# A GRU recurrence taken per half of its units, with the input products of 32 steps made at a time

## The chip, the core and the metric

One core of a Trainium2 chip runs the whole program. Its engines are named as the profile names them: PE (TensorE, the matmuls, with PEld for the weight loads that run beside them), DVE (VectorE), ACT (ScalarE), POOL (GpSimd) and SP (SyncE, which issues the transfers). The metric is the device time of one execution in microseconds, as the median over runs. Lower is better.

## What is computed

Four layers follow each other, each added to its input: two attention layers, a GRU over 256 time steps with 8 sequences and 512 units, and a layer with a norm. The change is in the third:

```python
def cell(h, x):
    gi = x @ W_ih + b_ih
    gh = h @ W_hh + b_hh
    i_r, i_z, i_n = jnp.split(gi, 3, axis=-1)
    h_r, h_z, h_n = jnp.split(gh, 3, axis=-1)
    r = jax.nn.sigmoid(i_r + h_r)
    z = jax.nn.sigmoid(i_z + h_z)
    n = jnp.tanh(i_n + r * h_n)
    h_new = (1.0 - z) * n + z * h
    return (h_new, h_new)
_, hs = jax.lax.scan(cell, initial_state, xs)
```

`r` is the reset gate, `z` the update gate, `n` the candidate. Each step needs the state of the step before, so 256 steps follow each other.

## The kernel before

The attention layers fill the first 926 us. Then comes `recurrent_and_last_layer`. Each of its 256 steps makes 48 recurrent products (L1003): for each of the three gates, four chunks of 128 of the 512 units of the state (`held`, the stationary side, 8 columns for the 8 sequences) times four blocks of 128 output units. The four blocks go to four groups of 32 partitions of one PSUM bank, so four products stand side by side in the array. The products are fp32; each is written once in the code and stands as two matmuls and two weight loads in the profile, so 48 are 96 and 96.

The banks are `psR` for reset (gate0), `psN` for the candidate (gate1) and `psZ`, two in turn, for the update gate (pg0, pg1). Before the recurrent products of the next step, `begin` (L1005) starts the update bank with its share of the input (`pick` times `foldZ`, L1018; in the first 16 steps L1016 in fp32) and the candidate bank with its bias (L1022), in bf16 of 128 columns.

DVE turns a bank by 32 x 32 blocks (STREAM_TRANSPOSE), so that units lie on the partitions, and then: reset turned (L896) and its input share added (L898), ACT's sigmoid (L951); candidate turned (L901), times reset (L905), plus its input share (L907), ACT's tanh (L953); update turned in two halves (L910, L911), two sigmoids (L956). The new state comes from two scans (L919), one for each half of the units. The next step's first products need the first half only; the wait for the second half stands after 12 of the 48 products.

Between the steps PE makes input products for later steps in the time that the chain leaves it: reset and candidate shares, 16 steps at a time (`TG`), 128 moving columns (`piece`, L977; ACT evicts them at L935), two pieces of four products a step; and update shares (`piece_z`, L987), one piece of four products a step, two in the first 16 steps. The shares of the first 16 steps are all made ahead of step 0. Pieces end 16 steps before the last step for reset and candidate and 32 steps before it for update. In the last 16 steps PE also makes column means for the last layer (L1059, L1066).

POOL adds the state to the residual stream (L855) and sums for the last layer (L859). Every engine runs its instructions in the order in which the code writes them, with semaphores between engines.

Of the kernel before, what the change touches and what calls it, by code (L numbers as in the profile page):

```python
# [680 lines left out]
def recurrent_and_last_layer(nc, xT, kept, loaded, w_hh, wk, wo, rowc, cols, out):  # L681
# [14 lines left out]
    with ExitStack() as ctx:  # L696
# [32 lines left out]
        def chunk(c, blk):  # L729
# [4 lines left out]
        tr = [trn[:, g, :].rearrange("p (c m) -> p c m", c=C)[:, :, 0:B] for g in range(GATES)]  # L734
# [3 lines left out]
        psZ, gb = pg[0:2], pg[2:4]  # L738
        (s_init, s_chain, s_gi_mm, s_gi_ev, s_acc, s_r, s_n) = (
            sem(n) for n in ("gates_cleared", "step_product", "gi_products",  # L740
                             "gi_ready", "state_added", "reset_ready", "candidate_ready"))
# [4 lines left out]
        R, Z, N = 0, 1, 2  # L746
        s_ps = [sem(f"gate_products{g}") for g in (R, N)]
        s_psz = sem("update_products")
        s_tr = sem("gates_turned")
        s_trz = [sem(f"update_turned{a}") for a in range(2)]  # L750
        s_pre = [sem(f"gate_summed{g}") for g in (R, N)]
        s_z = [sem(f"update_ready{a}") for a in range(2)]
        s_h = [sem(f"state_ready{a}") for a in range(2)]
        psR, psN, zb = ps
        NINIT = 22
        tR, tN = 0, 1


        TG, TZ, RZ = 16, 16, 3
        NG, PER = T // TG, 8  # L760
        gru = ctx.enter_context(ExitStack())

        near = gru.enter_context(nc.psum_tensor("near", [P, 512], fp32))
        turnedZ = [x[:, P:P + 64] for x in (psR, near)]
# [30 lines left out]
        T0 = T - TG  # L795
# [3 lines left out]
        with nc.Block() as block:  # L799
            @block.sync  # L800
            def _(sp):
# [8 lines left out]
                for n in range(1, NZ):  # L810

                    sp.wait_ge(s_part, 6 * n)
                    if n > RZ:

                        sp.wait_ge(s_psz, TZ * (n - RZ + 1))
# [46 lines left out]
            def _(dve):  # L862
# [5 lines left out]
                for bank in psZ:  # L868
                    dve.memset(bank[:, 0:P], 0.0).then_inc(s_init, 1)
                dve.memset(psN[:, 0:P], 0.0).then_inc(s_init, 1)  # L870
# [19 lines left out]
                for t in range(T):  # L890
# [4 lines left out]
                    dve.wait_ge(s_ps[tR], t + 1)  # L895
                    dve.transpose(trn[:, R, :], psR[:, 0:P]).then_inc(s_tr, 1)  # L896
                    dve.wait_ge(s_tr, 2 * t + 1)
                    dve.tensor_tensor(pre[:, 0], tr[R], share(t, R), ALU.add).then_inc(s_pre[tR], 1)  # L898

                    dve.wait_ge(s_ps[tN], t + 1)  # L900
                    dve.transpose(trn[:, N, :], psN[:, 0:P]).then_inc(s_tr, 1)  # L901

                    dve.wait_ge(s_tr, 2 * t + 2)
                    dve.wait_ge(s_r, t + 1)
                    dve.tensor_tensor(tmp[:], tr[N], rg[:], ALU.mult).then_inc(s_chain, 1)  # L905
                    dve.wait_ge(s_chain, t + 1)
                    dve.tensor_tensor(pre[:, 1], tmp[:], share(t, N), ALU.add).then_inc(s_pre[tN], 1)  # L907

                    dve.wait_ge(s_psz, t + 1)
                    dve.transpose(turnedZ[0], psZ[q][:, 0:64]).then_inc(s_trz[0], 1)  # L910
                    dve.transpose(turnedZ[1], psZ[q][:, 64:128]).then_inc(s_trz[1], 1)  # L911

                    for a in range(2):
                        dve.wait_ge(s_z[a], t + 1)
                        if a == 0:
                            dve.wait_ge(s_n, t + 1)
                            if t > 1:
                                dve.wait_ge(s_acc, t - 1)
# [8 lines left out]
            def _(a):  # L927
# [20 lines left out]
                for t in range(T):  # L948
                    q = t % 2
                    a.wait_ge(s_pre[tR], t + 1)  # L950
                    a.activation(rg[:], pre[:, 0], ACT.Sigmoid).then_inc(s_r, 1)  # L951
                    a.wait_ge(s_pre[tN], t + 1)
                    a.activation(sides[q][:, :, :, 0:3:2], pre[:, 1].rearrange("p c (b v) -> p c b v", v=1).to_broadcast([P, C, B, 2]), ACT.Tanh).then_inc(s_n, 1)  # L953
                    for z in range(2):
                        a.wait_ge(s_trz[z], t + 1)
                        a.activation(by[:, half(z), :, 2], turnedZ[z].rearrange("p (c m) -> p c m", c=H)[:, :, 0:B], ACT.Sigmoid).then_inc(s_z[z], 1)  # L956
# [11 lines left out]
            def _(pe):  # L968
# [31 lines left out]
                def products(bank, g, q, c, first, done, lo=0, hi=P):  # L1000
                    for j in range(4):
                        o = g * D + P * j
                        last = pe.matmul(bank[32 * j:32 * j + B, lo:hi], held[q][:, c, :], whh[:, c, o + lo:o + hi], start=first, stop=done)  # L1003
                    return last
                def begin(t):  # L1005

                    n, v = t // TZ, t % TZ
                    if t == 0:
                        pe.wait_ge(s_z0, 1)
                    elif n > 0 and v == 0:  # L1010
                        pe.wait_ge(s_zd[n % RZ], 192 * (n // RZ + (0 if n % RZ == 0 else 1)))
                    if t > 1:
                        pe.wait_ge(s_trz[1], t - 1)
                    for j in range(4):
                        if n == 0:
# [398 lines left out]
```

## Time and profile before

| | before |
|---|---|
| median of 3 runs | 1963.13 us (1960.36 to 1968.94) |
| profiled execution, span | 1963.7 us (the page gives no other time for it) |
| PE busy | 1832.6 us, 93% |
| PE weight loads busy | 1269.7 us, 65% |
| DVE busy | 1147.7 us, 58% |
| ACT busy | 785.3 us, 40% |
| mean granted TensorE clock | 0.968 |

Busy shares are over the whole span; the change touches only the stretch from 926 us on. In a table of stretches each engine has its busy time and, in brackets, its instructions. In a listing in order of time each row is a run of like instructions: start, length of the run, engine, line, operation, output and inputs, shapes, count, and in square brackets the idle time of the engine just before and what ended it. "issue" there means that nothing which the profile shows was waited for. PE's row and PEld's row of one line are the matmuls and the weight loads of the same products.

### The profile page before, as it was taken

To read this page: it belongs to the slowest core of one execution; us is meant where nothing else is said; L and a number is where in the kernel's file an instruction comes from. 1 tells how busy PE (TensorE), PEld (TensorE's weight loads), DVE (VectorE), ACT (ScalarE), POOL (GpSimd) and SP (SyncE) were. 2 spreads that over 40 slices of the span, in tenths; PEclk is the share of its full clock that TensorE was granted. 3 is DMA by queue.
4 is the path that set the end of the run, shared out by engine and by line. 5 is a ranking of instruction groups with operands and counts; after the bars stand their busy time and mean duration, and the time that the engine had idled before them with its cause. 6 is when DMAs were issued, how large, how long until landed. Compare 5 with 4: busy or idle time off the path is not lost. (4 is left out here: it accounts for less than half of the span.)

```text
span 1963.7 us, 85507 instructions
## 1 busy us (share of the span) xinstructions
PE 1832.6 (93%) x37682; PEld 1269.7 (65%) x37682; DVE 1147.7 (58%) x3364; ACT 785.3 (40%) x2196; POOL 393.5 (20%) x862
## 2 busy tenths in 40 slices
PE   6999999999999999988999999999999999999983
PEld 2433444453444344444998888888888999888861
DVE  5667676766676667343455555555555555555567
ACT  0554565655555565633222222222222222222224
POOL 0121211121111212110122122221222211222113
PEclk7997999999999999989999999999999999999995
DMA  6654443526152623141100000000000000000002
GB/s 160 219 141 126 121 127 85 152 63 181 47 172 67 180 68 93 34 152 42 77 15 10 13 13 13 13 4 13 13 13 13 7 11 13 13 13 12 5 4 86
DMA packets 65377, 127.65 MB, mean 65 GB/s; under 512 B 15401, under 2 KB 22057, under 8 KB 61412
## 3 DMA queue, kind: packets, MB, share of 16 engines
q1 hardware_dynamic: 61372, 120.30, 21.3%
q8 instruction: 296, 4.85, 1.0%
q0 software_dynamic: 3072, 0.82, 0.2%
q10 hardware_dynamic: 560, 1.05, 0.2%
q14 instruction: 77, 0.63, 0.1%
HBM read 77.56 MB, written 37.85 MB: 59 GB/s over the span
## 5 line engine op out<-in xcount | busy, mean ns | idle before, releaser
L439 DVE TENSOR_REDUCE mx<-MX 128x1 f32<-128x512 f32 x768 | 483.3, 683 | 191.7 <-PE MX L568 191.2
L1003 PE MATMUL gate<-whh,state 128*8 128x128 f32 x16384 | 503.8, 273 | 31.5 <-DVE state L919 13.4
L504 ACT ACTIVATE pr<-ST 128x512 f32<-128x512 f32 x768 | 409.5, 596 | 223.5 <-PE ST L588 223.1
L1003 PEld LDWEIGHTS gate<-whh,state 128*8 128x8 f32 x16384 | 430.4, 91 | 87.6 <-DVE state L919 84.7
L896 DVE STREAM_TRANSPOSE trn<-gate 128x128 f32<-128x128 f32 x256 | 81.3, 318 | 337.7 <-PE gate L1003 337.7
L1003 PE MATMUL pg<-whh,state 128*8 128x128 f32 x8192 | 278.4, 273 | 0.3 <-issue 0.3
L951 ACT ACTIVATE rg<-pre 128x32 f32<-128x32 f32 x256 | 58.8, 230 | 504.0 <-DVE pre L898 504.0
L568 PE MATMUL MX<-K,Q 51*128 51x512 f32 (+1 forms) x768 | 242.4, 445 | 15.0 <-DMA Q<-d_q 10.5
L588 PE MATMUL ST<-Q,K 53*128 53x512 f32 (+1 forms) x768 | 240.6, 485 | 13.3 <-ACT pr L504 9.2
L588 PEld LDWEIGHTS ST<-Q,K 53*128 53x128 f32 (+1 forms) x768 | 98.7, 189 | 215.5 <-ACT pr L504 118.9
L1003 PEld LDWEIGHTS pg<-whh,state 128*8 128x8 f32 x8192 | 230.3, 90 | 1.2 <-issue 0.9
L855 POOL TENSOR_TENSOR xT<-xT,state 128x32 f32<-128x32 f32 x256 | 67.4, 263 | 730.9 <-DVE state L919 730.9
L977 PE MATMUL pg<-xT,wih 128*32 128x128 f32 x4096 | 183.4, 276 | 12.0 <-issue 10.6
L568 PEld LDWEIGHTS MX<-K,Q 51*128 51x128 f32 (+1 forms) x768 | 121.1, 196 | 75.7 <-DVE mx L439 42.8
L382 POOL TENSOR_TENSOR nmp<-nm,zero 16x128 fp32r<-16x128 f32 x48 | 21.5, 448 | 629.3 <-ACT nm L520 629.3
L604 PE MATMUL AV<-pr,va 128*17 128x512 f32 x1024 | 139.0, 615 | 0.9 <-ACT pr L504 0.9
L977 PEld LDWEIGHTS pg<-xT,wih 128*32 128x32 f32 x4096 | 117.6, 110 | 25.3 <-issue 23.6
L953 ACT ACTIVATE state<-pre 128x64 f32<-128x64 f32 x256 | 66.5, 260 | 164.5 <-DVE pre L907 164.5
L919 DVE TENSOR_TENSOR_SCAN state<-by,state 128x48 f32<-128x48 f32 x512 | 104.5, 246 | 33.0 <-ACT by L956 0.5
L987 PE MATMUL gate<-wihZ,xT 128*32 128x128 f32 x2048 | 112.5, 273 | 1.4 <-PEq L33 1.4
L901 DVE STREAM_TRANSPOSE trn<-gate 128x128 f32<-128x128 f32 x256 | 81.0, 316 | 24.6 <-PE gate L1003 0.7
L910 DVE STREAM_TRANSPOSE gate<-pg 128x64 f32<-128x64 f32 x256 | 67.9, 265 | 24.8 <-PE pg L1003 0.6
(190 smaller groups left out, 1943.3 us busy)
## 6 DMA issues: line engine op xcount, KB each, us to landing
d_q<-hi_q SPq DMA_DIRECT2D x32, 256.0 KB, 3.5
d_q<-lo_q SPq DMA_DIRECT2D x32, 256.0 KB, 4.0
d_k<-hi_k SPq DMA_DIRECT2D x32, 256.0 KB, 2.9
d_k<-lo_k SPq DMA_DIRECT2D x32, 256.0 KB, 2.9
K<-d_k SPq DMA_DIRECT2D x64, 128.0 KB
Q<-d_q SPq DMA_DIRECT2D x64, 128.0 KB
K<-d_k SPq DMA_DIRECT2D x16, 512.0 KB
Q<-d_q SPq DMA_DIRECT2D x16, 512.0 KB
```

The lines of the kernel that those rows point to most:

```text
L439: dve.reduce_max(mx[:, u, col:col + 1], bank[:, :], AX.X).then_inc(mx_red, 1)
L504: act.activation(pr[:, kc % 2, i], ST[n % 3][:, :], ACT.Exp, scale=SCALE[UNITS[w][0]]).then_inc(exped, 1)
L568: pe.matmul(bank[:, :], Q[r, h, tok(qb)], K[r, h, :], start=True, stop=True).then_inc(mx_mm, 1)
L588: pe.matmul(ST[n % 3][:, :], K[r, h, tok(kc)], Q[r, h, :], start=True, stop=True).then_inc(st_mm, 1)
L604: last = pe.matmul(AV[r, :], v, pr[:, kc % 2, i, :], start=kc == 0, stop=kc == KC - 1)
L896: dve.transpose(trn[:, R, :], psR[:, 0:P]).then_inc(s_tr, 1)
L901: dve.transpose(trn[:, N, :], psN[:, 0:P]).then_inc(s_tr, 1)
L910: dve.transpose(turnedZ[0], psZ[q][:, 0:64]).then_inc(s_trz[0], 1)
L919: dve.tensor_tensor_scan(state[:, 1 - q, W3 * a:W3 * a + W3], by[:, half(a)].rearrange("p c b v -> p (c b v)"), threes(q, a), 0.0, ALU.mul ...
L977: last = pe.matmul(gb[i % 2][32 * j:32 * j + 32, 0:TG * B], wih[:, n, i * P + 32 * j:i * P + 32 * j + 32], xT[:, n, TG * blk:TG * (blk + 1 ...
L987: last = pe.matmul(zb[32 * j:32 * j + 32, P * w:P * (w + 1)], xT[:, k, t0:t0 + 4, :].rearrange("p t b -> p (t b)"), wihZ[:, k, P * w:P * ( ...
L1003: last = pe.matmul(bank[32 * j:32 * j + B, lo:hi], held[q][:, c, :], whh[:, c, o + lo:o + hi], start=first, stop=done)
```

## The change

The recurrent weights are put in another order on the host (`by_half`): the reset gate first, then for the first half of each 128-unit block its candidate and update columns side by side, then the same for the second half. A bank then holds 64 candidate and 64 update columns of one half: `psA` (gate1) for the first, `psB` (pg0, pg1 in turn) for the second. One step now makes reset and first-half products of the near chunks of the state, waits for the state's second half after 16 of the 48 products (before: 12), makes the far chunks of both, and then the whole second half. DVE turns each half's bank whole, and both the candidate's arithmetic and ACT's tanh run once for each half. The bank `near` goes.

The input shares of reset and candidate are made for 32 steps at a time (`TG` 32), 256 moving columns, one piece of four products a step instead of two; the first 32 steps' shares are made ahead of step 0, and the pieces end 32 steps before the last step. ACT's evictions come every fourth step instead of every second. Starting the banks takes 16 matmuls of 64 columns instead of 8 of 128.

```diff
-        TG, TZ, RZ = 16, 16, 3
+        TG, TZ, RZ = 32, 16, 3
...
+                    def turn(a):
+                        dve.wait_ge(s_ps[a], t + 1)
+                        dve.transpose(trn[:, a, :], half_bank(a, t)[:, 0:P]).then_inc(s_tr[a], 1)
+                    def candidate(a):
+                        dve.wait_ge(s_tr[a], t + 1)
+                        if a == 0:
+                            dve.wait_ge(s_r, t + 1)
+                        dve.tensor_tensor(tmp[:, half(a)], tr[a][:, 0:H], rg[:, half(a)], ALU.mult).then_inc(s_chain, 1)
+                        dve.wait_ge(s_chain, 2 * t + a + 1)
+                        dve.tensor_tensor(pre[:, 1, half(a)], tmp[:, half(a)], share(t, N)[:, half(a)], ALU.add).then_inc(s_pre[a], 1)
+                    def update(a):
                         dve.wait_ge(s_z[a], t + 1)
+                        dve.wait_ge(s_n[a], t + 1)
...
+                    turn(0)
+                    candidate(0)
+                    turn(1)
+                    update(0)
+                    candidate(1)
+                    update(1)
...
-                    if blk + 1 < NG and k % 2 == 1:
-                        keep(blk + 1, k // 2)
+                    if blk + 1 < NG and k % 4 == 3:
+                        keep(blk + 1, k // 4)
...
+                def begin(t, a):
...
                     for j in range(4):
+                        o = P * j + HW * a
+                        pe.matmul(bank[32 * j:32 * j + B, 0:HW], ones_b[:], bnp[:, o:o + HW], start=True, stop=False)
                     for j in range(4):
+                        o = P * j + HW * a
...
+                        pe.matmul(bank[32 * j:32 * j + B, HW:P], pick[:, B * (v % 4):B * (v % 4) + B], foldZ[:, n % RZ, v // 4, o:o + HW], start=False, stop=False)
...
                     if t > 0:
                         pe.wait_ge(s_h[0], t)
+                        pe.wait_ge(s_trr, t)
+                    products(psR, 0, q, NEAR, first=True)
+                    products(psA, 1, q, NEAR)
                     if t > 0:
                         pe.wait_ge(s_h[1], t)
+                    products(psR, 0, q, FAR, done=True).then_inc(s_psr, 1)
+                    products(psA, 1, q, FAR, done=True).then_inc(s_ps[0], 1)
+                    products(psB[q], 2, q, range(C), done=True).then_inc(s_ps[1], 1)
...
-                        piece(blk + 1, 2 * k)
-                        piece(blk + 1, 2 * k + 1)
+                        piece(blk + 1, k)
```

PE in one step of the recurrence, from the starting of the next step's banks to the update products. In these rows a fp32 product counts once. Before:

```order
L1018 MATMUL pg1<-foldZ,pick 8x128 [waits update_turned1]
L1018 MATMUL pg1<-foldZ,pick 8x128 x3
L1022 MATMUL gate1<-bnp,ones_b 8x128 [waits gates_turned]
L1022 MATMUL gate1<-bnp,ones_b 8x128 x3
L977 MATMUL pg2<-xT,wih_49 32x128 [waits gi_ready]
L977 MATMUL pg2<-xT,wih_49 32x128 x7
L987 MATMUL gate2<-wihZ,xT 32x128 x4
L1003 MATMUL gate0<-whh,state 8x128 [waits state_ready0]
L1003 MATMUL gate0<-whh,state 8x128 x7
L1003 MATMUL gate1<-whh,state 8x128 x4
L1003 MATMUL gate0<-whh,state 8x128 [waits state_ready1]
L1003 MATMUL gate0<-whh,state 8x128 x7
```

PE at the same place after the change:

```order
L1027 MATMUL gate1<-bnp,ones_b 8x64 [waits half_turned0]
L1027 MATMUL gate1<-bnp,ones_b 8x64 x3
L1033 MATMUL gate1<-foldZ,pick 8x64 x4
L1027 MATMUL pg1<-bnp,ones_b 8x64 [waits half_turned1]
L1027 MATMUL pg1<-bnp,ones_b 8x64 x3
L1033 MATMUL pg1<-foldZ,pick 8x64 x4
L984 MATMUL pg3<-xT,wih_49 32x256 [waits gi_ready]
L984 MATMUL pg3<-xT,wih_49 32x256 x3
L994 MATMUL gate2<-wihZ,xT 32x128 x4
L1011 MATMUL gate0<-whh,state 8x128 [waits reset_turned,state_ready0]
L1011 MATMUL gate0<-whh,state 8x128 x7
L1011 MATMUL gate1<-whh,state 8x128 x8
```

Sixteen narrow products start the banks instead of eight wide ones, four wide input products stand for eight, and the step's first product waits for two signals.

DVE in one step before, from the candidate's turning to the two scans (printed as SCALAR_TENSOR_TENSOR):

```order
L901 STREAM_TRANSPOSE trn<-gate1 128x128 [waits gate_products2]
L905 TENSOR_TENSOR tmp<-trn,rg 128x32 [waits reset_ready,gates_turned]
L907 TENSOR_TENSOR pre<-tmp,giT 128x32 [waits step_product]
L910 STREAM_TRANSPOSE gate0<-pg0 128x64 [waits update_products]
L911 STREAM_TRANSPOSE near<-pg0 128x64
L919 SCALAR_TENSOR_TENSOR state<-by,state 128x48 [waits state_added,candidate_ready,update_ready0]
L919 SCALAR_TENSOR_TENSOR state<-by,state 128x48 [waits update_ready1]
```

DVE at the same place after the change:

```order
L904 STREAM_TRANSPOSE trn<-gate1 128x128 [waits half_products0]
L910 TENSOR_TENSOR tmp<-trn,rg 128x16 [waits reset_ready,half_turned0]
L912 TENSOR_TENSOR pre<-tmp,giT 128x16 [waits step_product]
L904 STREAM_TRANSPOSE trn<-pg0 128x128 [waits half_products1]
L919 SCALAR_TENSOR_TENSOR state<-by,state 128x48 [waits state_added,candidate_ready0,update_ready0]
L910 TENSOR_TENSOR tmp<-trn,rg 128x16 [waits half_turned1]
L912 TENSOR_TENSOR pre<-tmp,giT 128x16 [waits step_product]
L919 SCALAR_TENSOR_TENSOR state<-by,state 128x48 [waits candidate_ready1,update_ready1]
```

The first half's scan now stands ahead of the second half's candidate, and behind the turning of the second bank.

## Rows read from the trace of the kernel before

**Rows 1.** The page: span, engines (busy us, share, instructions), a transfer queue (packets, MB).

```profile
span 1963.7 us, 85507 instructions
...
PE 1832.6 (93%) x37682; PEld 1269.7 (65%) x37682; DVE 1147.7 (58%) x3364; ACT 785.3 (40%) x2196; POOL 393.5 (20%) x862
...
q8 instruction: 296, 4.85, 1.0%
```

**Rows 2.** Table of stretches, reset transposes (L896) alone: one a step.

```profile
942.20:1006.50 64.30, 5.08 (x16) 1.00 0.04 12
1006.50:1787.10 780.60, 66.07 (x208) 1.00 0.04 11
1787.10:1903.00 115.90, 9.85 (x31) 1.00 0.03 8
```

**Rows 3.** Stretches: length, busy us and instructions of PE, PEld, DVE, ACT, POOL.

```profile
942.20:1006.50 64.30, 62.73 (x2252) 59.99 (x2242) 32.72 (x144) 18.15 (x75) 13.88 (x37) 1.00 0.04 12
1006.50:1787.10 780.60, 753.98 (x26627) 696.82 (x26624) 421.92 (x1873) 208.60 (x950) 174.38 (x494) 1.00 0.04 11
1251.90:1344.30 92.40, 87.72 (x3073) 80.96 (x3073) 48.80 (x217) 24.21 (x110) 20.93 (x58) 1.00 0.05 13
```

**Rows 4.** In order of time, one undisturbed step of the recurrence.

```profile
1058.64 1.65 PEld L1003 LDWEIGHTS gate<-whh,state 128*8 128x8 f32 x64 [0.40 <-DVE state L919]
1058.64 1.94 PE L1003 MATMUL gate<-whh,state 128*8 128x128 f32 x64
...
1059.99 0.32 DVE L896 STREAM_TRANSPOSE trn<-gate 128x128 f32<-128x128 f32 x1 [1.26 <-PE gate L1003]
...
1060.34 0.19 DVE L898 TENSOR_TENSOR pre<-trn,giT 128x32 f32<-128x32 f32 x1
1060.39 1.06 PE L1003 MATMUL pg<-whh,state 128*8 128x128 f32 x32
1060.56 0.23 ACT L951 ACTIVATE rg<-pre 128x32 f32<-128x32 f32 x1 [1.84 <-DVE pre L898]
...
1061.27 0.24 PE L1018 MATMUL pg<-foldZ,pick 96*8 96x128 bf16 x4
...
1061.38 0.62 PE L977 MATMUL pg<-xT,wih 128*32 128x128 f32 x16
1061.44 0.26 ACT L953 ACTIVATE state<-pre 128x64 f32<-128x64 f32 x1 [0.65 <-DVE pre L907]
1061.52 0.27 DVE L910 STREAM_TRANSPOSE gate<-pg 128x64 f32<-128x64 f32 x1
1061.69 0.22 DVE L911 STREAM_TRANSPOSE near<-pg 128x64 f32<-128x64 f32 x1
...
1062.04 0.41 DVE L919 TENSOR_TENSOR_SCAN state<-by,state 128x48 f32<-128x48 f32 x2
1062.35 0.23 PEld L1003 LDWEIGHTS gate<-whh,state 128*8 128x8 f32 x12 [0.40 <-DVE state L919]
```

**Rows 5.** In order of time, weight loads after a pause in three successive steps.

```profile
1274.48 0.25 PEld L977 LDWEIGHTS pg<-xT,wih 128*32 128x32 f32 x9 [0.66 <-issue]
...
1278.23 0.25 PEld L977 LDWEIGHTS pg<-xT,wih 128*32 128x32 f32 x9 [0.38 <-issue]
...
1282.25 0.25 PEld L977 LDWEIGHTS pg<-xT,wih 128*32 128x32 f32 x9 [0.66 <-issue]
```

**Rows 6.** Waits of weight loads (total us, times, longest): first 16 steps; then 208.

```profile
PEld gate L1003 <- issue: 1.8, 3, 0.8
...
PEld gate L1003 <- DVE state L919: 60.7, 164, 0.5
PEld pg L977 <- issue: 20.2, 46, 0.7
```

**Rows 7.** In order of time, PE's input products ahead of step 0.

```profile
934.22 5.37 PE L977 MATMUL pg<-xT,wih 128*32 128x128 f32 x128 [2.35 <-issue]
940.15 2.06 PE L977 MATMUL pg<-xT,wih 128*32 128x128 f32 x67 [0.56 <-issue]
```

More of the change, by code:

```diff
@@ L733, in recurrent_and_last_layer @@
         trn = sb("trn", [P, GATES, P])
-        tr = [trn[:, g, :].rearrange("p (c m) -> p c m", c=C)[:, :, 0:B] for g in range(GATES)]
+        tr = [trn[:, i, :].rearrange("p (c m) -> p c m", c=C)[:, :, 0:B] for i in range(3)]
         pre = sb("pre", [P, 2, C, B])
@@ L867, in _ @@
                 dve.memset(state[:], 0.0).then_inc(s_init, 1)
-                for bank in psZ:
+                for bank in psB:
                     dve.memset(bank[:, 0:P], 0.0).then_inc(s_init, 1)
-                dve.memset(psN[:, 0:P], 0.0).then_inc(s_init, 1)
+                dve.memset(psA[:, 0:P], 0.0).then_inc(s_init, 1)
                 dve.memset(ones_b[:], 1.0).then_inc(s_init, 1)
@@ L913, in _ @@
-                    for a in range(2):
+                    dve.wait_ge(s_psr, t + 1)
+                    dve.transpose(trn[:, 2, :], psR[:, 0:P]).then_inc(s_trr, 1)
+                    dve.wait_ge(s_trr, t + 1)
+                    dve.tensor_tensor(pre[:, 0], tr[2], share(t, R), ALU.add).then_inc(s_prer, 1)
+                    def turn(a):
+                        dve.wait_ge(s_ps[a], t + 1)
+                        dve.transpose(trn[:, a, :], half_bank(a, t)[:, 0:P]).then_inc(s_tr[a], 1)
@@ L998, in _, with products @@
                 pe.wait_ge(s_init, NINIT)
-                def products(bank, g, q, c, first, done, lo=0, hi=P):
-                    for j in range(4):
[L1002 to L1013, printed above, removed]
+                def products(bank, part, q, chunks, first=False, done=False):
+                    for c in chunks:
+                        for j in range(4):
+                            o = part * D + P * j
+                            last = pe.matmul(bank[32 * j:32 * j + B, 0:P], held[q][:, c, :], whh[:, c, o:o + P], start=first and c == chunks[0], stop=done and c == chunks[-1])
+                    return last
@@ new lines, in begin @@
+                def begin(t, a):
+                    n, v = t // TZ, t % TZ
+                    bank = half_bank(a, t)
+                    if a == 0:
+                        if t == 0:
+                            pe.wait_ge(s_z0, 1)
+                        elif n > 0 and v == 0:
+                            pe.wait_ge(s_zd[n % RZ], 192 * (n // RZ + (0 if n % RZ == 0 else 1)))
+                    if t > a:
+                        pe.wait_ge(s_tr[a], t - a)
+                    for j in range(4):
+                        o = P * j + HW * a
+                        pe.matmul(bank[32 * j:32 * j + B, 0:HW], ones_b[:], bnp[:, o:o + HW], start=True, stop=False)
@@ L1019, in begin @@
-                    if t > 0:
-                        pe.wait_ge(s_tr, 2 * t)
-                    for j in range(4):
-                        pe.matmul(psN[32 * j:32 * j + B, 0:P], ones_b[:], bnp[:, P * j:P * (j + 1)], start=True, stop=False)
-                begin(0)
+                        pe.matmul(bank[32 * j:32 * j + B, HW:P], pick[:, B * (v % 4):B * (v % 4) + B], foldZ[:, n % RZ, v // 4, o:o + HW], start=False, stop=False)
+                begin(0, 0)
+                begin(0, 1)
+                NEAR, FAR = range(H), range(H, C)
```

83 lines of the change are left out of this document (29 added, 54 removed).

## The prediction

> **What bounds the kernel now.** I read the page's head first, then the table of stretches, then one step in order of time, then the waits of the weight loads. The page [rows 1] gives 1963.7 us for the span and one number that decides this forecast: the queue of instruction packets moved 296 packets of 4.85 MB in all, 16 KB each, while PE ran 37,682 matmuls and 37,682 weight loads. 75,364 / 296 = 255, so one packet feeds about 256 PE instructions. I call that a block.
>
> The recurrence takes 256 steps, from about 942 to 1906 us. The count of reset transposes [rows 2] splits them: 16 first steps in 64.30 us (4.02 each), 208 steps in 780.60 us (3.753 each), then 31 in 115.9 us (3.74 each). In the 208 steps PE runs 26,627 + 26,624 instructions [rows 3], 256 a step, exactly one block a step.
>
> An undisturbed step [rows 4] takes 3.71 us (first product at 1058.64, next at 1062.35), and its end is a chain: 96 product matmuls, turn the update gate, sigmoid, scan, next product. PE idles 0.40 us on its weight port before the next step, until the scan lets it go. So the chain sets that step. Yet over the 208 steps the weight port sat idle 60.7 us for the scan and 20.2 us on "issue" [rows 6]: it waited for nothing the profile can name. Those pauses (46 of them) all stand at the input products, and in three successive steps they lie 3.75 and 4.02 us apart [rows 5]. Among the input products made ahead of the recurrence two such pauses stand exactly 128 matmuls, and so 128 loads, apart [rows 7]: the edge of a block. I read them as PE waiting for its next block of instructions. In the first 16 steps the weight port never waits for the scan; its waits are four lines of "issue", 3.5 us together, of which the longest stands in [rows 6]. PE is wanted all the time, at a granted clock of 1.00, and 2252 + 2242 instructions, 17.55 blocks, took 64.30 us: 3.66 us a block [rows 3].
>
> So there are three limits close together: the chain (3.71), PE's own work (below, 3.42), and the supply of blocks (3.66 and more).
>
> **The change part by part.** *The chain.* A group of four matmuls, one for each quarter of the partitions, takes 0.109 us (64 in 1.75 us, 1058.64 to 1060.39 [rows 4]). The reset transpose starts 1.35 us after the first product, 0.26 after its 40 matmuls are through. After the change reset is complete after 48: 1.31 + 0.26 = 1.57. Transpose to addition 0.35, addition to sigmoid 0.22, sigmoid 0.23 + 0.03: reset ready at 2.40. The first half's bank is complete after 64: 2.01, turned by 2.37. Product, addition and tanh of half the width: I take 0.22, 0.23 and 0.26 as for the full width (a little high): 3.1. On VectorE the scan of this half stands behind the transpose of the second bank, which waits for all 96 products (2.88). That transpose takes 0.32, but the row of the half transposes shows the next instruction 0.17 after one of 0.27, so the scan starts between 3.1 and 3.2. From scan to product 0.31: **3.41 to 3.51** against 3.71. The second half follows from 3.28 with product, addition, tanh and scan (0.22 + 0.22 + 0.26 and then 0.31), so PE sees its state at about 4.3; PE asks for it 32 matmuls after its own start, 0.87 us after 3.41 to 3.51, so at 4.28 at the earliest: in time, or 0.05 late.
>
> *PE's own work.* The weight port, idle for 0.40 until 1062.35, had its last load under way at 3.31 after the start [rows 4]; with one more group of 0.109 PE is through at 3.42 of 3.71. The starts of the banks go from two groups of 128 columns, 0.055 us each (1061.27 to 1061.38), to four groups of 64. No row shows 64 columns. If the columns set it, four cost the same 0.11; if each group has the price of the wide one, 0.22. So 0 to +0.11; I take +0.03, nearer the first, since the fp32 groups of [rows 4] too are paced by their columns (0.109 us for twice 0.055). The input products go from four groups of 128 columns to two of 256: columns alike, 0. PE's work is 3.41 to 3.53.
>
> *Instructions.* This is the term that counts. Of the rows PE runs in a step, 16 go with the input products (8 matmuls and 8 loads fewer) and 16 come with the halved starts. Still 256. The first product now waits for two signals; no row shows what a second wait is, and I count it as one instruction more: 257. In the first 16 steps, where the update share enters in fp32, 2 x 144 + 1 = 289 against 4494 / 16 = 281. So the change asks for 16 x 289 / 256 + 208 x 257 / 256 = 226.9 blocks where 844.9 us are spent today.
>
> *What a block costs* when PE wants it at once: 3.66 us in the first 16 steps, the only stretch where PE never waits for the chain; 3.753 over the 208 steps, which is too high as it holds the 60.7 us for the scan; 3.85 in the worst stretch of 92.4 us, 24.0 blocks [rows 3]. I take 3.71, between the first two. 226.9 x 3.71 = 841.8 us: **-3.1 us**. The chain's gain of 0.2 to 0.3 us a step turns into longer waits for blocks.
>
> The Trainium skill, "Runtime: NRT & Kernel Launch", section "Instruction fetch mechanics", says that instructions are refilled in blocks of 256, which the trace agrees with, and that crossing an edge is mostly hidden, since an engine dispatches more slowly than blocks arrive. The 20.2 us of "issue" speak against that second part here. By it the sum would be that of the first rival.
>
> *The last 32 steps* have no input products and no update products, so 224 + 1 instructions: a block lasts 1.14 steps, 3.71 / 1.14 = 3.26, under the chain. Here the gain is real: 3.74 - 3.47 = 0.27 in 28 of them. Three more hold a 512-column mean product, with which PE itself sets the step, and in the very last the second half ends about 0.4 later. 7.5 - 0.4 is about **-7.0**, bounds -2 and -9.
>
> *Ahead of the recurrence* the first input products now cover 32 steps: 256 matmuls of 256 columns, 64 groups at 0.213 instead of 0.109, +6.7. Among those of before PE idles 2.35 and 0.56 on issue [rows 7], which the longer work can fill: +6.7 - 2.9 = **+3.8**, bounds 0 and +7. ScalarE's evictions are half as many and twice as wide, VectorE has ten instructions a step for nine; both are idle for over a third of the 780.6 us [rows 3], so this costs 0 while PE sets the step; without that cover it is the 0.05 above.
>
> Sum: -3.1 - 7.0 + 3.8 = -6.3, on the profiled span of 1963.7: 1957.4. That span is 0.6 over the median of 1963.13, so **1957 us**.
>
> **The rivals.** *Blocks are not a limit.* Then a step takes the longer of chain and PE's work, 3.41 to 3.53, middle 3.47: 208 x (3.753 - 3.47) = 59 less, the pauses of 3.5 us in the first steps go too, and with -7.0 + 3.8 it is 1963.7 - 65.7 = 1898 us. For it: the undisturbed stretch has no pauses at 3.71 us a step. Against it: the first 16 steps, which want a block each 3.49 us (32 groups of 0.109) and get one each 3.66. The rule of the Trainium skill's "Runtime: NRT & Kernel Launch" given above is this rival's.
>
> *Blocks come as in the worst stretch.* After a pause PE has no lead, so the next block is late again; the intervals of 3.75 and 4.02 [rows 5] are then the rule. Today the wait for the scan gives a late block time to arrive; the change takes that wait away. At 3.85 a block: 226.9 x 3.85 = 873.6, +28.7, in all +25.5: 1989 us. The point of decision: with x us a block the sum is 226.9 x - 844.9 - 3.2; it is zero at 3.738, 0.5% over at 3.781 and 0.5% under at 3.695. Against it: that stretch is the worst of the trace.
>
> *The early start does not come.* The first half's scan stands behind the second bank's transpose. If the half-width steps cost more than I think and the chain stays at 3.71, the last steps gain nothing: 1964 us.
>
> **How the numbers follow.** 0.5% (about 10 us) is what a measurement of this kernel can tell from no change. Forecast (blocks at 3.66 to 3.78): 0.74, 1946 to 1973. Blocks no limit: 0.13. Blocks at 3.78 or more: 0.09. No early start: 0.04. Within the forecast I put 0.37 below 3.695. Faster: 0.13 + 0.74 x 0.37 = 0.40; slower 0.09; same the rest, 0.51. The range leaves out the first rival's 0.13 and the upper half of the second: 1938 to 1976.
>
> **What would show it.** In the changed profile: still one instruction packet for about 256 PE instructions; in the 208 steps 50 to 60 us of "issue" on the weight port instead of 20.2, and under 15 us for the scan instead of 60.7; the 208 steps in 765 to 785 us; the pauses no longer at one place in the step, since 257 instructions shift the edge by one each step; 31 last steps in about 109 us; the first product of the recurrence 4 us later. The forecast is wrong if issue time stays near 20 us while the scan's wait falls: then 1898 it is. It is wrong the other way if pauses of 4.02 follow each other through the stretch.

## The result: a little slower, 1.0068 of the time before

The changed kernel takes 1975.92 us (median of 20 runs) where the kernel before takes 1960.38 on the same chip (20 runs): a ratio of 1.0068, 95% interval 1.005 to 1.0086. In a second set of runs it was 1.0058 (1.0031 to 1.0084). So it is slower by some 6 to 17 us. The forecast was 1957 us, 6 less than before: the sign is wrong. The time lies inside the range that was given, 1938 to 1976, but only by 0.1 us, which is luck; by the prediction's own mark of 0.5% it is the outcome "slower", to which it gave 0.09.

The head of the page of the kernel after, to set beside [rows 1]:

```profile
span 1980.4 us, 86586 instructions
...
PE 1850.9 (93%) x37746; PEld 1216.0 (61%) x37746; DVE 1202.7 (61%) x3620; ACT 851.3 (43%) x2388; POOL 393.7 (20%) x862
...
q8 instruction: 297, 4.87, 1.0%
```

There are 64 matmuls and 64 loads more than before, and one packet more: still 75,492 / 297 = 254 PE instructions a packet. The stretches are those of [rows 2] (first 16 steps, 208 steps, the rest; the last row holds 32 reset turns here and 31 there, so the two aren't to be compared). Columns as in [rows 3]: length, busy us and instructions of PE, PEld, DVE, ACT, POOL, granted clock, DMA share, GB/s:

```profile
954.30:1019.00 64.70, 63.07 (x2312) 58.48 (x2302) 33.94 (x157) 21.29 (x85) 13.06 (x36) 1.00 0.04 11
1019.00:1803.00 784.00, 761.46 (x26649) 646.05 (x26643) 468.98 (x2083) 262.19 (x1106) 174.63 (x494) 1.00 0.05 11
1803.00:1919.00 116.00, 99.05 (x3578) 86.90 (x3574) 76.45 (x326) 37.72 (x161) 21.71 (x70) 1.00 0.03 8
```

The 208 steps take 784.0 us for 780.6, although PE's weight port is busy 51 us less than before. What it waits for in these steps (the five largest of eleven lines: total us, times, longest), beside [rows 6]:

```profile
PEld gate L1011 <- DVE state L919: 45.1, 158, 0.6
PEld gate L1027 <- DVE trn L904: 15.4, 33, 0.6
PEld pg L1011 <- issue: 7.2, 19, 0.7
PEld gate L1011 <- issue: 5.1, 14, 0.6
PEld pg L984 <- issue: 3.6, 9, 0.6
```

Before, all 46 pauses on "issue" stood at the input products. Now they stand at many places of the step (all lines of issue together 22.4 us). The second wait ahead of the step's first product (`s_trr`, L1041) stands in PE's queue as an instruction of its own, once a step, so that a step has 257; the kernel before has none there. In the 208 steps (line, times, ns, first and last start):

```profile
L1041 PEldq EVENT_SEMAPHORE  x208: 51/51/51, 1022.7 to 1802.2; - x104
```

With these counted, all 52 pauses of over 0.2 us on issue stand whole multiples of 256 instructions apart, to within one instruction. So they are edges of blocks.

There is also a new wait: PE starts a bank (L1027) and waits until VectorE has turned the first half (L904). Its cause is in the time order of a step. First an undisturbed step of the kernel after, beside [rows 4]:

```profile
1124.51 2.03 PE L1011 MATMUL gate<-whh,state 128*8 128x128 f32 x64
...
1126.15 0.32 DVE L897 STREAM_TRANSPOSE trn<-gate 128x128 f32<-128x128 f32 x1 [0.80 <-PE gate L1011]
...
1126.73 0.23 ACT L957 ACTIVATE rg<-pre 128x32 f32<-128x32 f32 x1 [1.36 <-DVE pre L899]
...
1127.46 0.32 DVE L904 STREAM_TRANSPOSE trn<-pg 128x128 f32<-128x128 f32 x1
1127.48 0.23 ACT L962 ACTIVATE state<-pre 128x32 f32<-128x32 f32 x1 [0.30 <-DVE pre L912]
...
1127.80 0.26 DVE L919 TENSOR_TENSOR_SCAN state<-by,state 128x48 f32<-128x48 f32 x1
...
1128.11 0.23 PEld L1011 LDWEIGHTS gate<-whh,state 128*8 128x8 f32 x12 [0.20 <-DVE state L919]
```

From first product to first product it is 3.60 us. The scan of the first half starts 0.34 after the second bank's transpose, when that has ended; and the reset turn starts 1.64 after the first product. Now a step in which GpSimd works on the update shares (L835):

```profile
1081.28 1.28 POOL L835 TENSOR_TENSOR giZ<-giZ,bz 128x512 f32<-128x512 f32 x1
1081.45 0.32 DVE L897 STREAM_TRANSPOSE trn<-gate 128x128 f32<-128x128 f32 x1 [0.87 <-PE gate L1011]
...
1081.80 0.81 DVE L899 TENSOR_TENSOR pre<-trn,giT 128x32 f32<-128x32 f32 x1
```

The reset addition, 0.19 us in the undisturbed step, takes 0.81 and ends as GpSimd's instruction ends (1082.61 and 1082.56). So it is with all 43 of these additions that take over 0.26 us: each ends 0.045 to 0.050 us after a long instruction of GpSimd. The transpose, which reads the bank, keeps its 0.32. Over all 256 steps the line's shortest, median and longest durations in ns are:

```profile
L899 DVE TENSOR_TENSOR pre<-trn,giT x256: 191/193/928, 956.4 to 1918.9; 128x32 f32<-128x32 f32 x128
```

It happens in three of every 16 steps. These take 4.24, 4.18 and 4.19 us on average, the other thirteen 3.56 to 3.73. GpSimd waits for the state's second half before it adds it up, and its long instruction stands behind those adds. The second half now comes later in the step, and so the long instruction falls on the reset addition, which is on the chain. In the kernel before, the two overlapped less: the additions of the 208 steps were lengthened by 5.0 us in all there, and by 25.1 here. This agrees with the Trainium skill, "SBUF — State Buffer", section "SBUF: two separate sides": a VectorE instruction with two SBUF inputs and a GpSimd instruction that reads SBUF exclude each other for their whole length.

So two things could hold the 208 steps at 784 us: the supply of instruction blocks (**theory B**), or the delays by GpSimd (**theory A**: 39 steps of about 0.6 us, some 25 us), without which the changed chain would have paid.

### The profile page after: what moved, and what is told of

Its sections match the earlier page's. It is cut to its first block and busy times, and to the rows that moved or that the text cites. A ratio compares the mean times of both kernels' runs of the same rounds, so it can differ in the third digit from the quotient of the medians.

```text
span 1980.4 us, 86586 instructions
## 1 busy us (share of the span) xinstructions
PE 1850.9 (93%) x37746; PEld 1216.0 (61%) x37746; DVE 1202.7 (61%) x3620; ACT 851.3 (43%) x2388; POOL 393.7 (20%) x862
## 5 line engine op out<-in xcount | busy, mean ns | idle before, releaser
L1011 PE MATMUL gate<-whh,state 128*8 128x128 f32 x16384 | 513.6, 273 | 26.2 <-DVE state L919 22.8
L1011 PEld LDWEIGHTS gate<-whh,state 128*8 128x8 f32 x16384 | 411.0, 91 | 103.7 <-DVE state L919 69.1
L1011 PE MATMUL pg<-whh,state 128*8 128x128 f32 x8192 | 285.7, 273 | 3.1 <-issue 2.7
L897 DVE STREAM_TRANSPOSE trn<-gate 128x128 f32<-128x128 f32 x256 | 81.2, 317 | 218.6 <-PE gate L1011 218.6
L919 DVE TENSOR_TENSOR_SCAN state<-by,state 128x48 f32<-128x48 f32 x512 | 131.5, 257 | 105.8 <-ACT state L962 94.2
L962 ACT ACTIVATE state<-pre 128x32 f32<-128x32 f32 x512 | 118.8, 232 | 166.0 <-DVE pre L912 166.0
L984 PE MATMUL pg<-xT,wih 128*32 128x256 f32 x2048 | 163.0, 381 | 1.5 <-issue 1.2
L960 ACT ACTIVATE by<-trn 128x16 f32<-128x16 f32 x512 | 114.9, 224 | 30.5 <-DVE trn L904 13.6
L910 DVE TENSOR_TENSOR tmp<-trn,rg 128x16 f32<-128x16 f32 x512 | 83.9, 164 | 35.8 <-ACT rg L957 1.0
L912 DVE TENSOR_TENSOR pre<-tmp,giT 128x16 f32<-128x16 f32 x512 | 89.6, 175 | 18.0 <-DVE tmp L910 0.4
```

Source lines behind the costliest of these rows:

```text
L912: dve.tensor_tensor(pre[:, 1, half(a)], tmp[:, half(a)], share(t, N)[:, half(a)], ALU.add).then_inc(s_pre[a], 1)
L960: a.activation(by[:, half(z), :, 2], tr[z][:, H:C], ACT.Sigmoid).then_inc(s_z[z], 1)
L962: a.activation(sides[q][:, half(z), :, 0:3:2], pre[:, 1, half(z)].rearrange("p c (b v) -> p c b v", v=1).to_broadcast([P, H, B, 2]), ACT.T ...
L984: last = pe.matmul(gb[i % 2][32 * j:32 * j + 32, 0:TG * B], wih[:, n, i * P + 32 * j:i * P + 32 * j + 32], xT[:, n, TG * blk:TG * (blk + 1 ...
L1011: last = pe.matmul(bank[32 * j:32 * j + B, 0:P], held[q][:, c, :], whh[:, c, o:o + P], start=first and c == chunks[0], stop=done and c == ...
```

## The experiments

**Take the delays away.** e1 makes the three long additions of GpSimd 16 columns wide and leaves the other columns out; e2 cuts them into quarters of 128 columns over more steps and computes everything.

```diff
e1
-  pool.tensor_tensor(giZ[1][:], giZ[1][:], bz[:, 0], ALU.add)
+  pool.tensor_tensor(giZ[1][:, 0:16], giZ[1][:, 0:16], bz[:, 0, 0:16], ALU.add)
...
-  pool.tensor_tensor(giZ[1][:], giZ[1][:], parts_z[:, i // 2 - 1], ALU.subtract)
+  pool.tensor_tensor(giZ[1][:, 0:16], giZ[1][:, 0:16], parts_z[:, i // 2 - 1, 0:16], ALU.subtract)
e2
+  PART_AT = [(j, w) for j in range(6) for w in (range(C) if j % 2 == 0 else (0,))]
...
+  c = slice(P * w, P * w + P)
...
+  pool.tensor_tensor(giZ[1][:, c], giZ[1][:, c], bz[:, 0, c], ALU.add)
...
+  pool.tensor_tensor(giZ[1][:, c], giZ[1][:, c], parts_z[:, j // 2 - 1, c], ALU.subtract)
```

> The changed kernel, but POOL's three additions and subtractions that split the update shares work on 16 of 512 columns (the other columns are left out, so the shares are incomplete). Theory A: these POOL operations hold up VectorE's reset addition in three steps of each 16 (4.28, 4.18 and 4.18 us a step against 3.56), 2.1 us for each 16 steps, 28 to 30 us in the 208 steps. Then the stretch shrinks from 783.7 to about 757 us, a little more than that if PE's waits for instructions rise, and the kernel is at 0.985 to 0.992 of the changed one, about 1948 us. Theory B (my prediction's: PE's supply of instruction blocks sets the pace at 3.71 us a step, and the long steps only stand where waits for blocks would stand otherwise): the stretch stays over 770 us, the kernel over 1964 us, and 'issue' idle on the weight port doubles from 22 us.

> The changed kernel with the same splitting work on POOL in full, but each addition and subtraction of 512 columns made as four of 128 columns, spread over 12 steps instead of 6. Theory A: each piece takes about 0.45 us and ends about when VectorE's reset addition starts, so the long steps go and the kernel is within 5 us of the narrow one, about 1950 us, faster than both given kernels. Theory B: no more than 5 us gained against the changed kernel. A rival within A, that the delay comes from the total time POOL works beside VectorE and not from where it falls: the four pieces cost as much as the one, spread out, and the kernel stays at about 1976 us.

e1: 1975.24 us, 1.0034 of before (1.0013 to 1.0055). e2: 1975.38 us, 1.005 (1.0028 to 1.0073). The 208 steps took 790.7 and 790.2 us, not fewer than in the kernel after. The waits of e1's weight loads in them:

```profile
PEld pg L1011 <- issue: 20.7, 45, 1.0
PEld gate L1011 <- DVE state L919: 20.4, 90, 0.6
PEld gate L1011 <- issue: 12.1, 31, 1.0
```

The waits for the scan have shrunk to 20.4 us, the wait for the turn is gone, and the nine-line list's eight lines of issue add up to 57.1. The delays were taken away and pauses for blocks took their place; all 114 of over 0.2 us stand multiples of 256 instructions apart. Theory A alone is out, and what was expected by theory B came (over 770 us, over 1964 us, issue more than doubled).

**Each part of the change alone.** e3 is the kernel after with 16-step input products (273 PE instructions a step instead of 257); e4 is the kernel before with 32-step products (240 instead of 256).

```diff
e3
-  TG, TZ, RZ = 32, 16, 3
+  TG, TZ, RZ = 16, 16, 3
...
-  piece(blk + 1, k)
+  piece(blk + 1, 2 * k)
+  piece(blk + 1, 2 * k + 1)
e4
-  TG, TZ, RZ = 16, 16, 3
+  TG, TZ, RZ = 32, 16, 3
...
-  piece(blk + 1, 2 * k)
-  piece(blk + 1, 2 * k + 1)
+  piece(blk + 1, k)
```

> The changed kernel with the input products of reset and candidate made 16 steps at a time with 128 columns, as before: the recurrence per half alone. PE then runs 273 instructions a step instead of 257. Theory A (blocks cost time only where PE asks for them faster than about one each 3.55 us): 273 instructions want a block each 3.34 us, so the undisturbed steps are held up too, at 3.6 to 3.75 us a block or 3.85 to 4.0 us a step, less what the POOL delays already cover: 208 steps take 790 to 815 us, 3.5 us come back ahead of step 0, and the kernel is at 1980 to 2000 us. Theory B, 3.71 us a block throughout: 3.96 us a step, 823 us, about 2010 us. If blocks cost nothing: 1972 us, only the start gained.

> The kernel before with the input products made 32 steps at a time, 256 columns, and nothing else: PE runs 240 instructions a step instead of 256 and wants a block each 3.96 us. Both theories: no 'issue' pauses in the steps, 208 steps at 3.72 us, 774 us instead of 781, and 3 to 4 us more ahead of step 0: about 1956 us, 0.996 to 1.000 of the kernel before. If the pauses are not the supply of instructions: the stretch stays at 780 us and the kernel is 3 us slower.

e3: 2030.75 us, 1.0309 (1.027 to 1.0348); the 208 steps 843.9 us. That is more than any of the three expectations allowed (2010 us at most): a block cost 3.804 us here, not 3.71. e4: 1956.37 us, 0.9947 (0.9918 to 0.9976); the 208 steps 773.0, as expected. All waits of e4's weight loads in its 208 steps are one line:

```profile
PEld gate L1003 <- DVE state L919: 84.9, 209, 0.5
```

No pause is left: at 240 instructions a step lasts 3.715 us, what the undisturbed step of [rows 4] takes. The second half of the change is a gain by itself. The first half, the recurrence per half, costs 63 us in the 208 steps, at 273 instructions each instead of 256.

**The count alone.** e8 adds 16 matmuls of one column to a step of e4 (272 instructions), e10 adds 8 to a step of the kernel after (273). e5 takes 16 instructions away from each step of the kernel after, from step 16 on: each half's bank is started by 4 matmuls of 128 columns, the candidate's bias rows beside the update's shares in one operand.

```diff
e8
+  if TZ <= t < T - 2 * TZ:
+      for i in range(16):
+          pe.matmul(psN[32 * (i % 4):32 * (i % 4) + B, 400:401], ones_b[:], bnp[:, 0:1], start=False, stop=False)
...
e10
+  if TZ <= t < T - 2 * TZ:
+      for i in range(8):
+          pe.matmul(psA[32 * (i % 4):32 * (i % 4) + B, 400:401], ones_b[:], bnp[:, 0:1], start=False, stop=False)
e5
...
+  for j in range(4):
+      o = P * (2 * j + a)
+      pe.matmul(bank[32 * j:32 * j + B, 0:P], pick[:, B * (v % 4):B * (v % 4) + B], foldZ[:, n % RZ, v // 4, o:o + P], start=True, stop=False)
+  return
...
```

> The kernel of e4 (before, with the 256-column input products alone, 240 TensorE instructions a step, 3.715 us a step, no pauses) and, in steps 16 to 223, 16 more matmuls of one column a step into a corner of a bank that nobody reads. They put nothing into the result and 32 instructions into a step: 272. Theory B (256 instructions of TensorE cannot be had faster than one block in 3.75 to 3.80 us): the step cannot be shorter than 272/256 of that, 3.98 to 4.04 us; 208 of them take 828 to 840 us where e4 took 773; the time is 2012 to 2024 us. Rival C (the count does not matter, only the work): 16 columns are under 0.02 us each by the nearest row (64 columns take 0.03 to 0.04), 0.3 us a step, and TensorE had 0.29 us a step to spare in e4: 1956 to 1966 us.

> The kernel after, but from step 16 on each half's bank is started by 4 matmuls of 128 columns instead of 8 of 64: the candidate's bias rows lie in the same operand as the update's shares. The result is the same; a step has 241 TensorE instructions instead of 257. Theory B (3.75 to 3.80 us per 256 instructions): the supply asks for 3.53 to 3.58 us a step, about what the undisturbed chain takes (3.556); the delays by GpSimd, hidden so far, now count, up to 28 us in the 208 steps; these steps take 742 to 772 us instead of 784 to 790, and the time is 1935 to 1960 us. Rival C (the count does not matter, work and chain do): eight short matmuls fewer are off the chain of the state, and the time stays at 1970 to 1980 us.

> The kernel after and, in steps 16 to 223, 8 more matmuls of one column a step into a corner of a bank that nobody reads: 273 TensorE instructions a step, as many as in e3, added in the way of e8. It tells what decides within the range that a block has cost so far. Theory B1 (a block of this kernel costs 3.75 to 3.80 us, as in e1, e2 and e3, and e8's 3.69 belongs to the kernel before, with its other order of waits): 4.00 to 4.06 us a step, 208 steps in 832 to 844 us, 2020 to 2035 us in all. Theory B2 (blocks with short added instructions come faster, as in e8): 3.69 us a block, 3.93 us a step, 818 us, 2005 to 2012 us. Rival C (the count does not matter): 0.15 us of work a step for an engine that already waits for the state in most steps: 1970 to 1985 us.

e8: 2000.84 us, 1.0194 (1.0153 to 1.0236); 208 steps in 815.2 us, 3.92 a step and 3.69 a block. Rival C (1956 to 1966) is out, and theory B's 2012 to 2024 was too much. The 16 matmuls came with 42 us in the 208 steps, and the pauses are back (45.4 us on seven lines in the 208 steps, of which two):

```profile
PEld gate L1003 <- issue: 17.7, 51, 0.7
PEld pg L1003 <- issue: 10.8, 28, 0.8
```

All 99 of over 0.2 us stand multiples of 256 instructions apart, which the work of the added matmuls would not bring about.

e10: 2021.07 us, 1.0272 (1.0238 to 1.0306); 208 steps in 833.1 us, 3.755 a block, as theory B1 said. Its 208 steps, then those of e5:

```profile
1010.70:1843.80 833.10, 780.89 (x28298) 692.40 (x28288) 459.64 (x2080) 262.60 (x1105) 173.62 (x494) 1.00 0.04 11
```

```profile
1014.60:1785.10 770.50, 752.08 (x24974) 628.48 (x24970) 471.55 (x2082) 261.59 (x1105) 173.90 (x494) 1.00 0.06 11
```

In e10 the weight port waits 81.4 us on issue. Eight matmuls of one column a step cost 45 us against e11's 788.6 (below) and 49 against the 784 of the first profile. e5: 1962.11 us, 0.9987 (0.9961 to 1.0012); 208 steps in 770.5 us, the upper end of what theory B expected (772; the whole time is 2 us over its 1960), and rival C is out. The starts of the banks themselves got no shorter. The starts of the banks in the kernel after (two of four rows), then in e6 (which starts them as e5 does), each with the products that follow, in order of time:

```profile
1078.83 0.21 PE L1027 MATMUL gate<-bnp,ones_b 96*8 96x64 bf16 x4
...
1078.87 0.21 PE L1033 MATMUL gate<-foldZ,pick 96*8 96x64 bf16 x4
...
1078.95 0.62 PE L984 MATMUL pg<-xT,wih 128*32 128x256 f32 x8
```

```profile
1300.46 0.24 PE L1047 MATMUL gate<-foldZ,pick 99*8 99x128 bf16 x4
...
1300.53 0.24 PE L1047 MATMUL pg<-foldZ,pick 99*8 99x128 bf16 x4
...
1300.58 0.61 PE L1001 MATMUL pg<-xT,wih 128*32 128x256 f32 x8
```

Both take 0.12 us to the next product (1078.83 to 1078.95, 1300.46 to 1300.58). What differs is the count, by 16 instructions a step. What e5's weight loads wait for in the 208 steps is now the state and, in 39 places, the turn that GpSimd delays:

```profile
PEld gate L1023 <- DVE state L931: 59.1, 208, 0.6
PEld gate L1042 <- DVE trn L916: 19.9, 39, 0.6
```

**Both limits away.** e6 is e5 with e2's quarters. e7 is e6 without PE's own wait for the reset turn and with update products of 256 columns, four of them every second step (232 instructions). e9 shares these out, two a step.

```diff
e7
...
-  Z_AT = [min(2 * t if t < TZ else TZ + t, len(PIECES_Z)) for t in range(T + 1)]
+  Z_AT = [min(t if t < TZ else (TZ + t) // 2, len(PIECES_Z)) for t in range(T + 1)]
...
-  wihZ[:, k, P * w:P * (w + 1)]
+  wihZ[:, k, 2 * P * w:2 * P * (w + 1)]
...
-  pe.wait_ge(s_trr, t)
e9
...
-  for j in range(4):
+  for j in (2 * y, 2 * y + 1):
...
```

> e5 with GpSimd's split additions cut to 128 columns as in e2. Theory B: supply 3.53 to 3.58 us, chain 3.556, and no long delays by GpSimd: 208 steps in 740 to 748 us, 1930 to 1945 us in all, 10 to 25 us less than e5 (where e2, with 257 instructions, gained nothing by the same cut). Rival C: like e2, 1970 to 1980 us. Rival D (the delays by GpSimd cost nothing with fewer instructions either): the time of e5.

> e6 without TensorE's own wait for the reset bank's turn (the wait for the state stands behind it anyway) and with the update gate's input products 256 columns wide: 4 of them every second step instead of 4 of 128 columns every step, 232 instructions a step. Theory B: supply 3.40 to 3.44 us, below the chain's 3.556, so that the chain sets the pace: 208 steps in 739 to 748 us, 1928 to 1945 us, level with e6 or up to 8 us faster; no issue pauses. If the 0.43 us of products that now fall on every second step get in the state's way there, up to 20 us more. Rival C: 1970 to 1980 us.

> e7 with the four wide update products of every second step shared out, two to each step: still 232 instructions a step, no uneven steps. In e7 the steps without these products take 3.52 to 3.54 us and those with them 3.64. If TensorE is late for the state only in the uneven steps: 3.53 to 3.56 us in all of them, 208 steps in 734 to 741 us instead of 747, 6 to 13 us less than e7 in all. Rival: the uneven steps lose it elsewhere or the chain's mean is what e6 and e7 both show (747 us): level with e7 within 3 us.

e6: 1934.61 us, 0.9847 (0.9805 to 0.9889); 208 steps in 747.0 us, inside theory B's range; rivals C and D are out. In e6, where GpSimd's piece is short, the reset addition keeps its 0.19 us (unlike 1081.80 above):

```profile
1302.98 0.46 POOL L854 TENSOR_TENSOR giZ<-giZ,bz 128x128 f32<-128x128 f32 x1
1303.05 0.32 DVE L914 STREAM_TRANSPOSE trn<-gate 128x128 f32<-128x128 f32 x1 [0.77 <-PE gate L1028]
...
1303.41 0.19 DVE L916 TENSOR_TENSOR pre<-trn,giT 128x32 f32<-128x32 f32 x1
```

e7: 1928.68 us, 0.981 (0.9762 to 0.9857), the lowest median of all, though its interval overlaps that of e6; 746.8 us for the 208 steps, one line of waits and no pause:

```profile
PEld gate L1028 <- DVE state L936: 94.0, 213, 0.8
```

e9: 1935.98 us, 0.9854 (0.9817 to 0.9891), 748.5 us for the 208 steps, where 734 to 741 were expected. Its rival holds for these steps: evening out the products gains nothing. The whole time is 7 us over e7's instead of within 3, with intervals that overlap. The steps of e7 with and without them average 3.59 us, the even steps of e9 3.60.

The four kernels e2, e5, e6 and the kernel after form a square:

| 208 steps, ratio of the whole time to before | GpSimd's additions in one piece | in quarters |
|---|---|---|
| 257 instructions a step | after: 784, 1.0068 | e2: 790, 1.005 |
| 241 instructions a step | e5: 771, 0.9987 | e6: 747, 0.9847 |

The rows of e2 and e6 for these steps (those of the other two are above):

```profile
1006.40:1796.60 790.20, 764.11 (x26636) 665.58 (x26625) 447.26 (x2080) 261.91 (x1105) 192.41 (x611) 1.00 0.05 11
```

```profile
1011.40:1758.40 747.00, 744.40 (x24970) 638.05 (x24963) 448.98 (x2081) 261.79 (x1105) 192.82 (x611) 1.00 0.07 12
```

Quarters alone gain nothing, fewer instructions alone 13 us in the 208 steps, both 37. I read it so: while blocks set the pace, the delays by GpSimd are time in which late blocks arrive; take the blocks away as a limit and the delays cost 24 us.

**Were the two first profiles typical?** e11 and e12 are the kernels after and before once more.

> The kernel after once more, unchanged, beside the kernel before, for a second profile. In its first profile the part ahead of the recurrence, whose instructions are those of before, ended 8.8 us later than in the profile of before, with more time at the lower granted clock, and the 208 steps took 783.7 us where the neighbours e1 and e2 took 790. If the first is a matter of the run: that part ends 0 to 5 us from before's 926.5 us. If the program causes it: again 7 to 11 us later. For the 208 steps: 790 us if a block's price is that of e1 and e2 (3.785), 784 if the delays by GpSimd give late blocks time to catch up and the price is 3.752.

> The kernel before once more, unchanged, for a second profile: the part ahead of the recurrence ends at 921 to 931 us and the 208 steps take 779 to 783 us, if the first profile was typical.

e11: 1980.2 us, 1.0058 (1.0031 to 1.0084). The part ahead of the recurrence ended at 921 us (935 in the first profile of after, 926.5 and 926.4 in the two of before), and in the ten profiles of e1 to e10 it ended at 921 to 930, so those 8.8 us were a matter of that one run. The 208 steps took 788.6 us, nearer to 790 than to 784. e12's 208 steps took 778.3, a little under the 779 to 783 expected. Its first 16 steps are the telling row, beside the first of [rows 3]:

```profile
942.39:1009.99 67.60, 64.70 (x2247) 60.52 (x2243) 32.68 (x144) 18.26 (x75) 13.82 (x37) 1.00 0.04 11
```

The same 16 steps of the same kernel took 67.60 us here and 64.30 there: 3.85 us a block (4490 / 256 = 17.54 blocks) against 3.66. No wait for the scan stands in them either; the longest entry of their list is

```profile
PEld gate L1003 <- issue: 3.5, 8, 0.8
```

## Why the prediction was wrong, point by point

**The step that failed is "What a block costs".** I took 3.71 us, between the 3.66 of the first 16 steps and the 3.753 of the 208 steps. The first row was one draw from a wide spread: in the second profile it was 3.85, and in the kernel after the first 16 steps took 3.58 (64.70 us) and 3.69 (67.04 us). And I called 3.753 too high "as it holds the 60.7 us for the scan". That does not follow: when that wait goes, the pause comes instead, as e1 shows. Where blocks set the pace in the 208 steps they cost 3.752 and 3.776 us (after, twice), 3.786 (e1), 3.783 (e2), 3.804 (e3), 3.755 (e10); only e8 had 3.69. With the 3.752 and 3.776 of the kernel after over the prediction's 226.9 blocks the term would have been +6.4 to +11.9 instead of -3.1. It measured +3.8 in the first pair of profiles and +9.8 in the second (first 16 and 208 steps together); it is less than the product because the first 16 steps of the kernel after had cheaper blocks. The text named the point of decision right: the sum is zero at 3.738.

**What bounds the kernel** was read right: one packet for 256 PE instructions, pauses at the edges, and three limits close together. The counting of the second wait as one instruction was right too. The Trainium skill, "Runtime: NRT & Kernel Launch", section "Instruction fetch mechanics", says that crossing an edge is mostly hidden. That does not hold here where a step wants 256 instructions or more: 16 more cost 45 to 49 us in the 208 steps (e10), 16 fewer gave 13 to 18 (e5), and the rival of 1898 us that went by this rule was not reached even by e7. In e4 and e7, where PE takes 3.96 us over a block, no pause is left.

**The chain** was mis-sized: 3.41 to 3.51 forecast, 3.53 to 3.60 measured (e6's steps have a median of 3.56, e7's without update products a mean of 3.53). Two terms: the reset turn starts at 1.64 instead of 1.57, and the scan starts 0.34 after the second bank's transpose, not 0.17; the overlap seen between two half transposes of [rows 4] isn't there between transpose and scan.

**GpSimd was missed.** I counted VectorE's tenth instruction as free while PE sets the step, and did not ask what GpSimd does when the state's second half comes later. In the kernel after this is hidden by the supply (e2 gained nothing), so it is not what turned the sign; in e5 it is worth 24 us. It also undoes the observation asked for, 50 to 60 us of issue and under 15 for the scan: after has 22.4 and 45.1, while e1, without the delays, has 57.1 and 20.4. By my own criterion ("wrong if issue time stays near 20 us ... then 1898") the profile of after would have read as the first rival: a small issue time was not a proof that blocks are no limit.

**Ahead of the recurrence:** +3.8 forecast, +3.2 and +2.8 measured (first update product to first recurrent product: 15.75 and 16.00 us before, 18.98 and 18.78 after). The sum is right, in part by luck. The longer products cost about the +6.7 forecast (64 groups at 0.216 us instead of 0.109), but the two pauses of [rows 7], 2.35 and 0.56 us on PE, are not filled: they have become one of 0.92 (0.72 in e11). What made up for it was not forecast: after its pause of 2.35 us the kernel before has 3.4 us (935.0 to 938.4) at a granted clock of 0.50, the lower of PE's two levels (1.2 and 2.4 GHz), in which four products of 128 columns take 0.213 us instead of 0.109; e12 has the same. After the shorter pause of the kernel after the clock stays at 1.00, in both profiles, which saves some 1.7 us. Before, then after (length, PE busy, granted clock, DMA share, GB/s):

```profile
934.20:938.40 4.20, 4.18 (x92) 0.59 0.93 390
```

```profile
938.70:942.40 3.70, 3.70 (x70) 1.00 1.02 430
```

The products of the kernel after, in order of time:

```profile
938.79 3.62 PE L984 MATMUL pg<-xT,wih 128*32 128x256 f32 x58
...
943.33 10.78 PE L984 MATMUL pg<-xT,wih 128*32 128x256 f32 x195 [0.92 <-issue]
```

**The last 32 steps:** -7.0 forecast, about -1.8 and -2.3 up to the start of the last step, and the last step itself about 0.6 longer (0.4 forecast). The mechanism was right, the size was off by the chain's 0.1 us and by GpSimd's three delays in the first 16 of them. What follows the recurrence took another 1.4 to 2.2 us more than before; e4, whose last steps are those of before, shows 1.1 to 1.8 of it too, so the recurrence per half isn't the cause of most of it. I leave it open.

**All parts together** come to some 8 us in the first pair of profiles and 12 in the second, where -6 was forecast; the block term is the largest part of the miss. The medians differ by 15.5 and 9.4 us; no run splits the rest. The part ahead of the recurrence alone ended anywhere from 921 to 935 us in these profiles.

**Pauses at many places in the step** came as forecast: with 257 instructions a step the edge moves by one each step. **Bank starts:** four of 64 columns take 0.12 us, the low end of the 0.11 to 0.22 given.

**What a block's time is made of** the records of the packets show. Wherever two pauses on issue stand at successive edges, exactly one packet of 16 KB lies between them (85 times in e1). It starts 1.26 us after the first load behind the edge, takes 1.20, and PE's next block begins 1.42 after its end (medians in e1; 1.31, 1.17 and 1.40 in before). So no second block is under way there, and I read the price as the time of one such round.

**Open:** why that round is longer in one stretch than in another, 3.58 to 3.85 us on average. e8 and e10 add the same kind of instruction and differ (3.69 and 3.755), so it isn't how short the added ones are.

## What to carry to other kernels

Count the instructions of an engine that never rests: here 256 PE instructions, however short, took about 3.75 us (3.58 to 3.85 by stretch), and fusing or widening matmuls pays even where their work stays the same. When several limits lie within a few per cent of each other, taking one away moves the waiting to the next; only the square of both changes showed what each was worth. Where a chain is moved within a step, look at every instruction on GpSimd that then falls beside a VectorE instruction with two SBUF inputs, and take a price from more than one stretch and more than one profile.

## What the hardware showed that I had not expected

An addition of 32 columns on VectorE took up to 0.93 us instead of 0.19 because a GpSimd addition of 512 columns had begun before it; a transpose that reads a bank, beside the same GpSimd instruction, kept its 0.32. Eight matmuls of one column cost 0.21 to 0.24 us a step. And the same 16 steps, some 4490 PE instructions, took 64.30 us in one execution and 67.60 in another, at a granted clock of 1.00 in both.
